# The low parts of the loaded queries: made by VectorE instead of GpSimd in a merged attention loop

## The reference, cut to what matters

```
x = x + attention(gate1(x, fside, cond))      # 16 heads of 128, causal
x = x + experts(gate2(x, fside, cond))        # 32 experts, 6 of them per token, and a shared one

gate(r, k):   two scans over the 512 tokens, forwards and backwards, of exp(k)*k and of exp(k)
              out = sigmoid(r) * numerator / denominator * factor
attention(x): q = (x @ Wq + bq).reshape(b, 16, 512, 128)    # not a split of the columns into heads
              k, v = x @ Wk + bk, x @ Wv + bv, split by columns into 16 heads
              softmax(q k^T / sqrt(128) + causal mask) v, @ Wo + bo
```

## Time and profile before

| | |
|---|---|
| median of 3 runs | 2662.51 us (2656.43 to 2663.44) |
| profiled execution, its own time | 2666.88 us |
| its span in the trace | 2664.7 us |
| mean granted clock of TensorE | 0.93 |
| TensorE busy | 2283.1 us, 86% |
| VectorE busy | 1200.3 us, 45% |
| ScalarE busy | 1123.1 us, 42% |
| GpSimd busy | 1425.9 us, 54% |
| DMA | 382 MB, 143 GB/s over the span |

### The profile page before, as it was taken

How to read it: one execution, slowest core, us unless ns; L and a number is a source line. 1 busy time by engine, 2 the same in 40 slices (tenths; PEclk the granted TensorE clock), 3 DMA queues, 4 the chain that set the end, 5 groups by cost and what they waited for, 6 DMA issues and landing times. The chain is left out here.

```text
span 2664.7 us, 41295 instructions
## 1 busy us (share of the span) xinstructions
PE 2283.1 (86%) x11897; PEld 1923.5 (72%) x11899; DVE 1200.3 (45%) x1953; ACT 1123.1 (42%) x2440; POOL 1425.9 (54%) x993
## 2 busy tenths in 40 slices
PE   1558999999999999998379649999999799999676
PEld 1336888788888887777257428999998789999554
DVE  7335777777755555665452002222222122222355
ACT  2226677676766666666221003233333223333211
POOL 5447766766755555454014754444449976520276
PEclk6678999999999999999779759999999899999788
DMA  1445444644464444431423554444446655422366
GB/s 46 123 139 158 141 140 139 198 140 141 137 203 130 129 130 153 116 117 50 171 79 113 214 189 140 146 144 144 131 149 205 210 182 174 152 90 74 112 200 186
DMA packets 284719, 381.97 MB, mean 143 GB/s; under 512 B 19909, under 2 KB 176649, under 8 KB 280649
## 3 DMA queue, kind: packets, MB, share of 16 engines
q1 hardware_dynamic: 230280, 262.16, 32.7%
q10 hardware_dynamic: 38976, 68.17, 7.6%
q0 software_dynamic: 15360, 50.34, 5.9%
HBM read 247.17 MB, written 133.43 MB: 143 GB/s over the span
## 5 line engine op out<-in xcount | busy, mean ns | idle before, releaser
L1585 POOL TENSOR_TENSOR we_low<-we_raw,we_high 128x1408 fp32r<-128x1408 f32 (+1 forms) x96 | 317.7, 3310 | 8.0
L1583 POOL TENSOR_SCALAR we_high<-we_raw 128x1408 fp32r<-128x1408 f32 (+1 forms) x96 | 135.2, 1408 | 320.5 <-PE up_e L365 315.4
L1693 DVE TENSOR_TENSOR hT_low<-hT_ps,hT_high 128x256 fp32r<-128x256 f32 x127 | 54.0, 425 | 390.2 <-ACT hT_high L1659 390.2
L365 PE MATMUL gate_e<-we_high,xT_high 128*128 x508 | 177.8, 350 | 28.2 <-POOL we_low L1585 27.8
L1706 DVE TENSOR_TENSOR hidden_e<-silu_e,up_e 128x352 f32<-128x352 f32 x127 | 66.2, 521 | 293.1 <-ACT silu_e L1670 293.1
L1670 ACT ACTIVATE silu_e<-gate_e 128x352 f32<-128x352 f32 x127 | 59.0, 465 | 326.3 <-PE up_e L365 326.3
L365 PE MATMUL proj<-c_high,wQ_high 128*128 128x512 f32 x256 | 114.0, 446 | 64.6 <-POOL wQ_low L585 64.6
L1675 ACT ACTIVATE rows_out<-down_e 128x512 f32<-128x512 f32 x127 | 76.0, 599 | 216.5 <-PE down_e L365 216.5
L365 PE MATMUL gate_e<-we_high,xT_low 128*128 x508 | 166.2, 327 | 0.0
L365 PE MATMUL gate_e<-we_low,xT_high 128*128 x508 | 165.9, 327 | 0.0
L365 PE MATMUL up_e<-we_high,xT_high 128*128 x508 | 164.2, 323 | 0.0
(11 more groups left out here) (294 smaller groups left out, 7172.6 us busy)
## 6 DMA issues: line engine op xcount, KB each, us to landing
slots_in<-zero_row SPq DMA_DIRECT2D x80, 416.0 KB
rows_in<-slots_in ACTq DMA_DIRECT2D x129, 256.0 KB, 2.8
slots_out<-rows_out ACTq DMA_DIRECT2D x127, 256.0 KB, 2.1
we_raw<-L_ffn_w_gate SPq DMA_DIRECT2D x32, 704.0 KB, 4.5
we_raw<-L_ffn_w_up SPq DMA_DIRECT2D x32, 704.0 KB, 5.1
w_ring<-L_attn_Wq SPq DMA_DIRECT2D x64, 256.0 KB, 3.6
q_T<-q_out SPq DMA_DIRECT2D x64, 256.0 KB, 2.8
w_ring<-L_attn_Wv SPq DMA_DIRECT2D x64, 256.0 KB, 3.7
```

The source lines that it names most:

```text
L365: last = nc.tensor.matmul(out, a, b, start=start and i == 0, stop=stop and i == len(terms) - 1)
L1583: nc.gpsimd.tensor_scalar(wh[:, p, at:to], raw[:, at:to], 1.0, 1.0, ALU.mult, ALU.mult).then_inc(w_hi, 1)
L1585: nc.gpsimd.tensor_tensor(wl[:, p, at:to], raw[:, at:to], wh[:, p, at:to].bitcast(F32), ALU.subtract).then_inc(w_split, 1)
L1693: nc.vector.tensor_tensor(htl[:, 0:2, :], psh[:, 0:2 * P].rearrange("p (c t) -> p c t", c=2), hth[:, 0:2, :].bitcast(F32), ALU.subtract)
```

## The change

The first `split_queries` below is in GpSimd's block, the second in VectorE's. The four subtractions per pass move from GpSimd's queue to VectorE's. Their operation, operands and semaphores stay the same. In VectorE's order `h0` stands ahead of `O0` and `h1` behind `O1`, both ahead of the reciprocals of the second gate; `r2` and `r3` stand around `gR`, the second half of the reciprocal of the first gate. In GpSimd's order they are taken out, and the rest keeps its order.

```diff
@@ -317,8 +317,8 @@
-DVE_ORDER = "M0 ga i0 V0 gb V1 V2 a0 M1 i1 V3 gd gr b0 gR gf K2 a1 M2 A0 b1 ha i2 K3 hb A1 M3 a2 i3 b2 k0 A2 a3 b3 gm k1 A3 O0 hd O1 hr hR hf O2 O3".split()
-POOL_ORDER = "u u u s1 u u u r2 r3 u u u u u cl u s2 u u u h0 p2 p1 u h1 p3".split()
+DVE_ORDER = "M0 ga i0 V0 gb V1 V2 a0 M1 i1 V3 gd gr b0 r2 gR r3 gf K2 a1 M2 A0 b1 ha i2 K3 hb A1 M3 a2 i3 b2 k0 A2 a3 b3 gm k1 A3 h0 O0 hd O1 h1 hr hR hf O2 O3".split()
+POOL_ORDER = "u u u s1 u u u u u u u u cl u s2 u u u p2 p1 u p3".split()
...
-            def split_queries(n):
-                pool.wait_ge(q_hi, n + 1)
-                tt(head(ql, n), head_raw(n), head(qh, n).bitcast(F32), ALU.subtract).then_inc(q_lo, 1)
...
+            def split_queries(n):
+                dve.wait_ge(q_hi, n + 1)
+                tt(head(ql, n), head_raw(n), head(qh, n).bitcast(F32), ALU.subtract).then_inc(q_lo, 1)
...
-                    if kind == "h":
+                    if kind == "h" and e[1] not in "01":
                         if it >= 0:
                             gate2(e, it)
+                        continue
+                    if e in ("r2", "r3") and it >= 0:
+                        split_queries(HG * it + int(e[1]))
+                        continue
+                    if e in ("h0", "h1"):
+                        if 0 <= it + 1 < NIT:
+                            split_queries(HG * (it + 1) + int(e[1]))
                         continue
```

More of the change, by code:

```diff
@@ L625, in _ @@
                         split_low(unit_of(it, next(units)))
[L626 to L629, removed]
                     elif e == "s1" and it < NFIRST:
```

## The result

The changed kernel takes 2670.04 us (median of 13 runs, 2664.18 to 2674.81) against 2660.88 us for the kernel before on the same chip (13 runs, 2656.43 to 2666.48): a ratio of 1.0035, with a 95% interval of 1.0024 to 1.0045, some 9.2 us slower. The forecast was 2671 us, slower by 8.5 us from a median of 2662.51 us.

A forecast was written before the change was run, and what follows sets the result against it. TensorE was taken as the bound, waiting for VectorE and hardly for GpSimd. Mid-pass 6.4 us plus end-of-pass 1.8 us gave 8.2, rounded to 8.5: 2671 us from the median of 2662.51 us; range 2659 to 2687 us.

The forecast's parts named there:

- a free h1: Start of a pass, h1 costing VectorE nothing: wK_low done by 370, worth 3 us (2659 us).
- the low end: Lowest price of one moved subtraction on VectorE: 0.69 us, as for contiguous inputs, against the 1.05 us taken.
- third rival: Start of a pass: GpSimd's backlog goes away and V2's stall with it, 10 us less, 2652 us; chance 0.12.
- part 1: End of a pass (h0, h1), 7 times: V0 loses 0.1 us, V2's stall grows by 0.25 us; 1.8 us.
- Part 2: Middle of passes 0 to 7 (r2, r3): K2 and a1 late, b1 loses 0.8 us each; 6.4 us.
- Part 3: Later passes (8 to 15): nothing lost, 0.3 us of cover at V0; if gone, V0 loses 1.05 us, 8 times.
- second rival: Strided read on VectorE dearer, up to 1.57 us, delays in all three places: together 24 us, 2687 us; chance 0.22.
- Pass 0: Start of the first pass: S0 somewhat sooner, but V0 needs wV_low, which waits for h1; nothing net.
- The signs: What would show it: q_low near 1.05 us, a new b1 wait, v_low waits of 1.5 us, GpSimd down 105 us.
- The first: VectorE's subtraction takes 0.69 us, as for contiguous inputs: 1 to 2 us in sum, 2664 us; chance 0.18.
- the fourth: Middle of a pass: turns fall so that r2 and r3 cost 0.3 us or less; within 3 us, 2664 us; chance 0.06.

The follow-up runs named there:

- the kernel without low parts: Against the kernel before, no engine makes the queries' low parts and the scores' third product rereads the high part; 0.9988, 3.0 us less.
- The contiguous kernel: Changed kernel with VectorE's subtraction reading a contiguous piece instead of elements 512 bytes apart; 1.0009, +3.3 us on before.
- h1_twice: Changed kernel with one more subtraction of the same size ahead of h1 in passes 8 to 14; 1.0127 on before, +34 us by the ratio.
- v0_first: Against a kernel with all four subtractions on VectorE and r3 ahead of K3, V0's low part moved ahead of the first gate's scans; 1.0102, +26 us on before.

## Why the prediction was right

The mechanism and both places were right, and the sum came out for the reason given. Small parts of the agreement are luck, named below.

**Who waits.** The step on which all rests, that TensorE waits for VectorE and hardly for GpSimd, is shown by the kernel without low parts: 3 us for all of GpSimd's relief. The prediction had "3 us" for a free h1.

**The price.** Taken as 1.05 us from a reduction with a stride; the median is 1.11 us, 1.09 over the 27 that had no GpSimd instruction beside them. The 0.1 us of fixed cost in that working is shown by no run; all instructions here have one length, so the measured 1.09 us can't be split. The contiguous kernel shows the low end at 0.69 us. The formula of the Trainium skill (VectorE: DVE Perf Modes, the section on the TRN2 errata) holds for that one and fails for the strided one by 0.4 us; the rule on lines of 16 bytes in the Trainium skill's SBUF — State Buffer points the right way. The third rival set 0.69 against 1.57 us as VectorE's advantage, a contiguous instruction against a strided one; like against like it is 0.69 to 1.29 us, and 1.10 to 1.57 us for the one that was moved.

**Turns with GpSimd.** h1 started at 362.55 while dk ran until 363.18, and ended at 364.05, 0.87 us later (predicted 0.85); GpSimd's ekv ended at 365.15, 1.1 us after that, as predicted. With the 3.43 us between the two S0 added, the worked-out times meet the trace of that pass to 0.1 us up to the second scan: hf 367.37 (measured 367.35), O2 368.11 (368.13), nf 370.90 (370.92), end of the second scan 375.00 (375.10); with part 1's 0.33 us added too, r2 389.88 (389.88), r3 393.09 (393.07), a1 396.5 (396.29).

**Part 1.** Predicted 0.1 us at V0 and 0.25 at V2, measured 0.27 and 0.33. V0 started 0.18 us after O2's read had ended; that handover was not in the working. The term was 1.8 us in sum; at 0.33 us in each of seven passes it is 2.3.

**Part 2.** Predicted 0.8 us, measured 0.82; which of r3 and gf waits for wV_low was left open, and it was gf (393.96, 1.74 us).

**Part 3.** Predicted: hf at 905.85 in the old times, 0.2 us ahead of wO_low. Measured from S0: 905.76. The doubled h1 shows that the cover is as thin as stated, and that its loss costs far more than the 1.05 us per pass of the second rival: the step counted one instruction, not a second turn with GpSimd or the clock.

**Pass 0.** Its start was taken as nothing net, as S0 comes sooner by about what h1 costs. In fact V0 waits for wV_low behind h1 there, 0.35 us more than S0 gains; with b1's 0.82, which was in the sum, that pass costs 1.2 us. The sum was 8.2 us, and the 0.3 us that rounded it to 8.5 "for the first pass" had no working behind it: that they match this 0.35 us is luck, as is some of the nearness of 2671 to 2670.04 us, since the forecast started 1.6 us above the median that before has over 13 runs and fell 0.7 us short in the slowdown.

**The signs.** One of them failed as it was written. V2's wait should have grown to 1.5 us, and a wait that shrinks was to prove the prediction wrong; it reads 1.25 us, 8.4 us in sum against 8.9. V2 is later all the same, by 0.33 us from S0. The wait didn't show it because V0, from whose matmuls it is counted, is itself 0.27 us late, and because it is 0.9 us in pass 4, where before has 1.64. The start from S0 should have been the sign. GpSimd's busy time fell by 98 us, not 105, and passes 8 to 11 last 66.05 us, not 68.

**The rivals.** The first (0.69 us, 1 to 2 us in sum) is ruled out by the duration; the contiguous kernel gives it 3.3 us (0.0 to 4.8 by the ratio). The second had the right direction, but 1.11 us is far from 1.57. The third falls with the kernel without low parts, and the fourth with the 0.82 us of part 2.

## What to carry to other kernels

An engine that is busy for 45% of the span, and for 74% of a gated pass, may have no room: what counts is the slack of the one consumer behind each place in its queue, here 1.65 us at b1 and 0.3 us at V0. An instruction with two inputs in SBUF must be priced with its turn against GpSimd (up to 1.05 us more here, 1.79 against 0.75 us for hf) and with its stride. When a moved instruction's delay is moved away, ask which wait is next: here it went from b1 to S3 to b2. In this kernel the work was best left on GpSimd, for which TensorE hardly waits, though GpSimd takes 1.57 us for it and VectorE 1.10.

## What the runs showed of the hardware

- VectorE's subtraction of 128x512 with one input in steps of 512 bytes takes 1.09 to 1.11 us, contiguous 0.69 us; GpSimd takes 1.57 us for the strided one against 1.29 for a contiguous one.
- VectorE with two SBUF inputs and GpSimd take turns by whole instructions: 0.87 us of VectorE's 1.10 come after GpSimd's end, and GpSimd's next ends 1.1 us after VectorE's.
- Before the change, TensorE's stalls at V2 (1.2 to 1.64 us in passes 1 to 6) left the granted clock at 1.00. Around one of 2.26 us at the start of passes 9 to 15 of h1_twice, and around one of 2.23 us in passes 1 to 7 of v0_first, it fell to 0.50 for 3.4 us in five of seven cases each, and stayed at 1.00 in the other two. Where it fell, the delay grew by another 1.3 to 1.7 us.
